# Leaving one low half out of a ternary weight: 23 matmuls in place of 24 in each split product of a decoder kernel

## The reference

```
def _ternary_dequant(w):                       # w is (1024, 1024); groups of 128 along a row
    wg = w.reshape(O, g, 128)
    scale = clip(mean(abs(wg), axis=-1, keepdims=True), 1e-8)
    wn = wg / scale
    q = where(wn > 0.5, 1.0, where(wn < -0.5, -1.0, 0.0))
    return (q * scale).reshape(O, I)
def _bitlinear(x, w): return x @ _ternary_dequant(w).T

x = x + self_attention(layernorm(x), w_q, w_k, w_v, w_o)    # each projection a _bitlinear; rope on q and k
x = x + cross_attention(layernorm(x), ctx, ctx)
x = x + experts(layernorm(x), A, B, Wr, br)
```

## Time and profile before

| | |
|---|---|
| median of 3 runs | 2347.63 us (2345.82 to 2349.23) |
| profiled execution, its own time | 2352.2 us |
| its span in the trace | 2350.4 us |
| granted TensorE clock, mean | 0.97 |
| first half ends, second begins | about 1657 us into the span |

### The profile page before, as it was taken

How to read it: one execution, slowest core, us unless ns; L and a number is a source line. 1 busy time by engine, 2 the same in 40 slices (tenths; PEclk the granted TensorE clock), 3 DMA queues, 4 the chain that set the end, 5 groups by cost and what they waited for, 6 DMA issues and landing times. The chain is left out here.

```text
span 2350.4 us, 52152 instructions
## 1 busy us (share of the span) xinstructions
PE 2135.3 (91%) x19912; PEld 1386.6 (59%) x19912; DVE 1640.3 (70%) x4559; ACT 1143.4 (49%) x2562; POOL 919.3 (39%) x855
## 2 busy tenths in 40 slices
PE   1565999999999999999999999998789998989988
PEld 1343666666666666666666666665445555555544
DVE  9997567667676676676676766655577777777764
ACT  7976433333333333333333333333666766666661
POOL 1111333333333333333333333332555565565650
PEclk9777999999999999999999999998899999999999
DMA  9976555656556555556465555558977868696852
GB/s 243 194 154 146 118 138 129 155 118 149 137 130 136 141 130 142 127 139 146 120 153 133 130 137 138 122 128 219 223 168 171 201 172 206 165 205 155 190 122 68
DMA packets 741961, 358.16 MB, mean 152 GB/s; under 512 B 688200, under 2 KB 688456, under 8 KB 741712
## 3 DMA queue, kind: packets, MB, share of 16 engines
q1 hardware_dynamic: 741712, 354.82, 64.2%
HBM read 104.11 MB, written 49.28 MB: 65 GB/s over the span
## 5 line engine op out<-in xcount | busy, mean ns | idle before, releaser
L819 POOL TENSOR_TENSOR halves<-prob,halves 128x384 f16<-128x384 f32 x256 | 234.6, 916 | 725.1 <-ACT halves L762 725.1
L62 PE MATMUL ps_j<-xT,wT 128*128 128x256 f16 x3744 | 428.3, 275 | 50.6 <-DMA wT<-rows_qkv 50.6
L87 DVE CUSTOM_DVE_ANT_0 prob<-ps_s,mask 128x128 f32<-128x128 f32 (+1 forms) x1024 | 304.6, 353 | 225.3 <-PE ps_s L77 224.2
L62 PEld LDWEIGHTS ps_j<-xT,wT 128*128 128x128 f16 x3744 | 368.8, 99 | 112.5 <-issue 50.6
L93 ACT ACTIVATE prob<-prob,negmax 128x128 f32<-128x128 f32 x512 | 202.0, 395 | 285.0 <-DVE negmax L87 284.8
L939 DVE TENSOR_TENSOR raw<-raw,cos 128x512 f32<-128x512 f32 x128 | 137.9, 1077 | 290.5 <-DMA swp<-raw 290.5
L62 PE MATMUL ps_t<-xT,wT 128*128 128x256 f16 x2400 | 270.2, 273 | 0.0
L62 PEld LDWEIGHTS ps_t<-xT,wT 128*128 128x128 f16 x2400 | 234.5, 98 | 38.2
L94 ACT ACTIVATE prob<-prob,negmax 128x256 f32<-128x256 f32 x512 | 252.9, 494 | 0.0
L1441 POOL TENSOR_TENSOR halves<-prob,halves 128x768 f16<-128x768 f32 x128 | 210.5, 1645 | 91.7 <-ACT halves L1385 91.6
L752 ACT ACTIVATE raw<-ps_j 128x512 f32<-128x512 f32 x78 | 46.4, 595 | 408.9 <-PE ps_j L62 408.9
(11 more groups left out here) (186 smaller groups left out, 3644.9 us busy)
## 6 DMA issues: line engine op xcount, KB each, us to landing
swp<-raw SPq DMA_DIRECT2D x512, 64.0 KB, 2.0
xin<-in_x SPq DMA_DIRECT2D x33, 512.0 KB, 4.2
kv_ahead<-in_ctx SPq DMA_DIRECT2D x16, 1024.0 KB, 5.5
x_kept<-after_self_attention SPq DMA_DIRECT2D x16, 1024.0 KB, 5.6
xres<-in_x SPq DMA_DIRECT2D x31, 512.0 KB, 4.1
after_self_attention<-xres SPq DMA_DIRECT2D x30, 512.0 KB, 3.3
queries<-q2T SPq DMA_DIRECT2D x30, 512.0 KB, 3.1
out<-x SPq DMA_DIRECT2D x10, 1024.0 KB, 4.6
```

What stands on the lines that cost most here:

```text
L62: last = pe.matmul(out, lhs(i, a), rhs(j, a), start=a == 0 and k == 0, stop=a == n_tiles - 1 and k == 2)
L87: dve.tensor_tensor_reduce(scores[:, cols], bank[:, cols], hidden, scale, NO_SCORE, ALU.add, ALU.min, least[:, n:n + 1]).then_inc(done, 1)
L819: pool.tensor_tensor(halves[:, e, 1, :], prob[:, e], halves[:, e, 0, :], ALU.subtract).then_inc(prob_lo, 1)
```

## The change

Each row of a weight matrix is multiplied with a ratio that makes the scale of its first group a float16 number: ratio = float16(256 s0) / (256 s0). The first group then has no low half, a weight tile has 15 blocks and not 16, and a product needs 23 matmuls. The result of a row is divided by its ratio afterwards.

- `ternary(n)`: one operation on 24 values (`bounds`) in place of three of the four of L862, then a reciprocal and a float16 copy of the first scale, their product (`ratio`), the scales times the ratio (`scaleR`), and the reciprocal of the ratio (`factor`). High and low halves of the scales are two operations on GpSimd (`halves_of_scales`), placed in its order beside the tiles.
- `scaled_rows(n)`: 15 activations.
- q and k: `projection` becomes two activations of 256 columns, each with its factor per partition as scale; the rotary tables are divided by 256 once, on GpSimd.
- v and the output product: the factors run along columns there, so they go out to DRAM and come back to all partitions (`store_factors`, `load_factors`, three times), and one more VectorE operation multiplies the bank in PSUM with them (`scaled_values`, the first operation of `add_projection`). `low_values` moves behind `maxima`, `high_values` on ScalarE behind `projection` and the step's first weight tile.
- In SBUF `swp` moves beside `cos` and `sin`, the weights shrink by a sixteenth, and some small tiles are joined.

```diff
-def split_product(pe, out, lhs, rhs, n_tiles, part=None):
+def split_product(pe, out, lhs, rhs, n_tiles, part=None, exact=None):
     for a in part or range(n_tiles):
-        for k, (i, j) in enumerate(((0, 1), (1, 0), (0, 0))):
-            last = pe.matmul(out, lhs(i, a), rhs(j, a), start=a == 0 and k == 0,
-                             stop=a == n_tiles - 1 and k == 2)
+        terms = [t for t in ((0, 1), (1, 0), (0, 0)) if a > 0 or exact is None or t[exact] == 0]
+        for t in terms:
+            last = pe.matmul(out, lhs(t[0], a), rhs(t[1], a), start=a == 0 and t is terms[0],
+                             stop=a == n_tiles - 1 and t == (0, 0))
...
+            def store_factors(k):
+                m, cols, rows = factor_part(k)
+                sp.wait_ge(factor_done, number[2 + m, cols.stop - 1] + 1)
+                with nc.allow_non_contiguous_dma("one column"):
+                    sp.dma_start(factors[m, rows].rearrange("(t p) -> p t", p=P),
+                                 factor_vo[:, m, cols]).then_inc(factor_out, 16)
+            def load_factors(k):
+                m, cols, rows = factor_part(k)
+                sp.wait_ge(factor_out, 16 * (k + 1))
+                sp.dma_start(factor_rows[:, m, rows], factors[m, rows].partition_broadcast(P)) \
+                    .then_inc(factor_in, 16)
...
-                for i, scale in ((0, scaleW), (1, low)):
+                for i, scale in ((0, scaleR), (1, low)):
...
-                    for g in range(NG):
+                    for g in range(i, NG):
...
-                act.activation(raw[:, g % 2].rearrange("p w n -> p (w n)"), bank(("qk", g, 0))[:],
-                               ACT.Copy, scale=1.0 / W_SCALE).then_inc(raw_done, 1)
+                for w in range(2):
+                    last = act.activation(raw[:, g % 2, w], bank(("qk", g, 0))[:, bass.ts(w, T)],
+                                          ACT.Copy, scale=factor_qk[:, w, t:t + 1])
+                last.then_inc(raw_done, 1)
...
+            def halves_of_scales(n):
+                u = n % NS
+                pool.wait_ge(scales_done, n + 1)
+                pool.tensor_tensor(high[:, u, :], bounds[:, u, 0, :],
+                                   ratio[:, u:u + 1].broadcast_to([P, NG]), ALU.mult) \
+                    .then_inc(high_done, 1)
+                pool.wait_ge(high_done, n + 1)
+                pool.tensor_tensor(low[:, u, :], scaleR[:, u, :], high[:, u, :],
+                                   ALU.subtract).then_inc(low_done, 1)
...
+            pool.wait_ge(tables_in, 32)
+            for table in (cos, sin):
+                pool.tensor_scalar(table[:], table[:], 1.0 / W_SCALE, None, ALU.mult) \
+                    .then_inc(tables_done, 1)
...
-                for to, factor, bound in ((scaleW, W_SCALE, ALU.max), (high, W_SCALE, ALU.max),
-                                          (thr[:, :, 0], 0.5, ALU.max),
-                                          (thr[:, :, 1], -0.5, ALU.min)):
-                    dve.tensor_scalar(to[:, u, :], asum[:, u, :], factor / GROUP,
-                                      factor * SCALE_EPS, ALU.mult, bound).then_inc(scaled, 1)
-                dve.wait_ge(scaled, 4 * n + 4)
-                dve.tensor_tensor(low[:, u, :], scaleW[:, u, :], high[:, u, :],
-                                  ALU.subtract).then_inc(low_done, 1)
+                dve.scalar_tensor_tensor(
+                    bounds[:, u], asum[:, u, :].unsqueeze(1).broadcast_to([P, 3, NG]),
+                    SCALE_EPS * GROUP, parts.unsqueeze(2).broadcast_to([P, 3, NG]),
+                    ALU.max, ALU.mult).then_inc(scaled, 1)
+                dve.wait_ge(scaled, n + 1)
+                dve.reciprocal(inverse0[:, u:u + 1], bounds[:, u, 0, 0:1]).then_inc(first_done, 1)
+                dve.tensor_copy(high0[:, u:u + 1], bounds[:, u, 0, 0:1]).then_inc(first_done, 1)
+                dve.wait_ge(first_done, 2 * n + 2)
+                dve.tensor_tensor(ratio[:, u:u + 1], high0[:, u:u + 1], inverse0[:, u:u + 1],
+                                  ALU.mult).then_inc(ratio_done, 1)
+                dve.wait_ge(ratio_done, n + 1)
+                dve.tensor_scalar(scaleR[:, u, :], bounds[:, u, 0, :], ratio[:, u:u + 1], None,
+                                  ALU.mult).then_inc(scales_done, 1)
+                factor = factor_qk[:, m] if m < 2 else factor_vo[:, m - 2]
+                dve.reciprocal(factor[:, t:t + 1], ratio[:, u:u + 1]).then_inc(factor_done, 1)
...
+            def scaled_values(c):
+                half = c[2] % 2
+                dve.wait_ge(j_ready, ready(c))
+                dve.wait_ge(factor_in, 16 * (half + 1))
+                dve.scalar_tensor_tensor(bank(c)[:], bank(c)[:], 1.0 / W_SCALE,
+                                         factor_rows[:, 0, bass.ts(half, BANK)],
+                                         ALU.mult, ALU.mult).then_inc(v_scaled, 1)
...
-                dve.scalar_tensor_tensor(z, bank(c)[:], 1.0 / W_SCALE, z, ALU.mult, ALU.add) \
-                    .then_inc(freed(c)[0], 1)
+                dve.wait_ge(out_scaled, 4 * c[1] + c[2] + 1)
+                dve.tensor_tensor(z, bank(c)[:], z, ALU.add).then_inc(freed(c)[0], 1)
...
-                    low_values(extra[g - 1])
+                    scaled_values(extra[g - 1])
...
                     maxima(g - SCORES)
+                if g - 1 in extra and extra[g - 1][0] == "v":
+                    low_values(extra[g - 1])
```

More of the change, by code:

```diff
@@ L180, in self_attention @@
     stats = sb("stats", [P, 2, 6])
[L181 to L184, removed]
+    small = sb("small", [P, 8])
+    minus_half, nothing = small[:, 0:1], small[:, 1:2]
+    rstd, mv = small[:, 2:3], small[:, 3:5]
+    parts = small[:, 5:8]
     NS = 4
     asum = sb("asum", [P, NS, NG])
-    scaleW = sb("scaleW", [P, NS, NG])
+    bounds = sb("bounds", [P, NS, 3, NG])
+    high0 = sb("high0", [P, NS], F16)
+    inverse0 = sb("inverse0", [P, NS])
+    ratio = sb("ratio", [P, NS])
+    factor_qk = sb("factor_qk", [P, 2, DT])
+    factor_vo = sb("factor_vo", [P, 2, DT])
+    scaleR = sb("scaleR", [P, NS, NG])
     high = sb("high", [P, NS, NG], F16)
     low = sb("low", [P, NS, NG])
-    thr = sb("thr", [P, NS, 2, NG])
     def staging(name, slots, pairs):
@@ L769, in _ @@
             for g in range(GEND):
-                if g - 1 in extra and extra[g - 1][0] == "v":
-                    high_values(extra[g - 1])
                 if 0 <= g - SUMS - 1 < GP:
@@ L777, in _ @@
                     scaled_rows(n)
+                if g - 1 in extra and extra[g - 1][0] == "v":
+                    high_values(extra[g - 1])
                 if 0 <= g - SCORES < GP:
@@ L850, in ternary, with compare @@
                 stage, below, sign, _ = staged(n)
+                m, t = tiles[n]
                 u = n % NS
                 w = stage.rearrange("p (g i) -> p g i", g=NG)
+                def compare(to, k, side):
+                    dve.tensor_tensor(to.rearrange("p (g i) -> p g i", g=NG), w,
+                                      bounds[:, u, k, :].unsqueeze(2)
+                                      .broadcast_to([P, NG, GROUP]), side).then_inc(compared, 1)
                 dve.wait_ge(*weights_loaded(n))
@@ new lines, in ternary @@
+                dve.tensor_scalar(scaleR[:, u, :], bounds[:, u, 0, :], ratio[:, u:u + 1], None,
+                                  ALU.mult).then_inc(scales_done, 1)
+                factor = factor_qk[:, m] if m < 2 else factor_vo[:, m - 2]
+                dve.reciprocal(factor[:, t:t + 1], ratio[:, u:u + 1]).then_inc(factor_done, 1)
+                compare(below, 2, ALU.is_lt)
+                before = n - 2 if n < NQKV else n - 1
+                if before >= 0 and n != NQKV:
+                    dve.wait_ge(halved, 2 * before + 2)
@@ L874, in ternary @@
+                compare(sign, 1, ALU.is_gt)
                 dve.wait_ge(compared, 2 * n + 2)
```

141 lines of the change are left out of this document (95 added, 46 removed).

## The result

The changed kernel takes 2327.37 us (median of 4 runs, 2324.65 to 2333.75) against 2347.77 for the kernel before (4 runs), a ratio of 0.9907 with a 95% interval of 0.9889 to 0.9925. On another chip the same pair gave 0.9924 (0.9906 to 0.9942). The forecast of 2322 and its range hold, but two of its terms were wrong and partly cancelled. The profiled execution took 2324.65, its span is 2322.5.

A forecast was written before the change was run, and what follows sets the result against it. VectorE was taken to bound the start, TensorE the middle stage. Saving -51.0, start +19.6, late rotation +4, seam +1 and second half +1 make -25.4 us: from 2347.6 to 2322, range 2304 to 2340.

The forecast's parts named there:

- Rival 4: Whole kernel: a matmul less gives back no time since weight loads set the pace, leaving only costs, 2373 us; chance 0.01.
- The late rotation (+4): Middle stage: `rotated` has little room, some steps will be late by a few tenths; +4 us, bounds 0 and 17.
- rival 2: Middle stage: GpSimd's subtraction slides, rotation sets the pace, TensorE waits 0.3 us in 56 steps; 17 us, 2335; chance 0.17.
- rival 3: VectorE's turn in every step: rewriting a PSUM bank is slow, about 2370 us at 2.4 us an operation; chance 0.05.
- The start (+19.6): First stage, where VectorE is the path: all additions there, (a) to (e), cost 19.6 us.
- (a): Start, VectorE's chain of small operations: 0.37 us more a tile, 28 tiles, 10.4 us, bounds 6 to 19.
- (b): Start: GpSimd's halves of the scales hold VectorE's compare, 0.25 us a tile, 7.0 us, bounds 0 and 12.4.
- (c): Start: value results need two VectorE operations in place of one, 4.1 us, of which 2.1 counts.
- (d): Start: ScalarE's rows end 0.3 us sooner in three waits, -0.9 us.
- (e): Start: rotary tables divided on GpSimd once, beside compares, 1.0 us, bounds 0 and 2.
- The stores: Start, SyncE's queue: three 4-byte-element stores and three loads cost nothing, hidden by VectorE work; without that about 4 us each.
- Rival 1: Start nearly free: (a) at its lower bound 7, (b) nothing, (c) 2; -43 us in all, 2305; chance 0.13.

The follow-up runs named there:

- only-saving kernel: The kernel before with the first tile's low-half matmul left out of every q, k, value and output product, nothing else changed: 2304.22 us, ratio 0.9791.
- kernel with only the costs: The changed kernel with all 24 matmuls a product again: 2384.42 us, ratio 1.0129 to the kernel before.
- contiguous stores: The changed kernel with factors stored in 16 or 32 bytes per partition, so in another order: 2312.75 us, ratio 0.9819; again 2315.09 us, 0.9833.
- kernel without the ratio's operations: The kernel with contiguous stores, without VectorE's operations for ratio and factor (both set to 1 once): 2303.33 us, ratio 0.9782 to the kernel before.

## Why the prediction was right, and where it was not

**The saving (-51.0) was right.** The only-saving kernel gives 49.6 in all. In the changed kernel 48.5 lie between pairs 12 and 127, 0.42 a step in the mean and 0.43 from pair 51 to 75, where 0.438 was forecast. Columns explain it: 1024 columns in 0.43 us are 0.42 ns each, which is one cycle at 2.4 GHz, the level that the granted clock of 1.00 stands for. Rival 4 fell.

**The late rotation (+4) was over-sized, and rival 2 fell.** In seven or eight of the 114 steps between pairs 12 and 127 the scores wait for `rotated`, about 1 us together (read from the starts in the timeline), and the middle stage is 0.6 us longer than in the only-saving kernel. `projection`'s two activations of 0.468 take 0.84 together, not 0.90, and GpSimd's subtraction did not become the pace. The kernel with only the costs shows a middle stage unchanged to 0.1 us.

**The rewritten bank takes 0.692**, forecast 0.69; rival 3 fell. VectorE has 78 of 100 us, forecast 77.

**The start (+19.6) came out at +22.7, with another make-up.**

- (a), the small operations, had the chain right and its worth too dear: 0.91 in place of 0.54 for a tile, as forecast. Over all 32 tiles the time from the end of the sum to the start of the compare, worked out from the timeline, adds up to 35.5 us after and 23.1 before. But all that VectorE and GpSimd add moves pair 12 by no more than 7.4 to 7.6 us with contiguous stores, less than the 10.4 of (a) alone. The 11.7 us of the kernel without the ratio's operations aren't a measure of the 10.4, since its chain is shorter than that of the kernel before, too.
- (b), "I take 0.25: 28 x 0.25 = 7.0", is a step that failed. The compares keep 1.21 and 1.22 us, and GpSimd's operations wait for them. The earlier trace rows had shown a compare that began 0.06 behind a GpSimd operation and took 1.94; I carried that over to operations that begin behind the compare. The Trainium skill ("SBUF — State Buffer", section "Who interferes with whom") is right in that the two exclude each other and the later one blocks; in this kernel the later one is GpSimd's, so its 12.4 us never arise. Where GpSimd holds the first turn the old picture is seen (timeline of both engines):

```profile
118.52 2.13 POOL L885 TENSOR_TENSOR xh<-xin,xh 128x1024 f16<-128x1024 f32 x1 [4.41 <-ACT xh L792]
...
119.83 0.86 DVE L960 SCALAR_TENSOR_TENSOR bounds<-asum,small 128x24 f32<-128x24 f32 x1
```

- (c), (d) and (e) weren't measured one by one. Of what (a) adds, 4.1 us come back in the compares themselves, which the forecast didn't look for: before, four of them lasted 1.94 to 3.15 us, one of them shown in the earlier trace rows, and now none takes more than 1.23 (without the ratio's operations three take 1.93 again, so it goes by where GpSimd's long operations happen to fall). What is left, 12.4 less 4.1, is 8.3, close to the 7.4 to 7.6 measured, so (c) and (e) can't be large. How (c), (d) and (e) share the small rest stays open.
- The stores, "in SyncE's queue I cost at nothing, hidden by the 10 us of VectorE work between", is the other step that failed. They cost 15.3 us here (22.7 less 7.4, by kernels from two chips) and 21.9 on the second chip (pair 12 at 315.2 less 293.3, both from there). I asked whether the factors come in time, and they do. What isn't hidden is what is in flight or queued behind the store, the transposes above all: they hold the weights, the layer norm tiles and, through the queue's order, the swapped halves on which the scores wait. Even the 4 us of "without that cover about 4 us each" was under half of what the third store cost, 9.4 us: from pair 9 to 12 the changed kernel takes 48.0 us, with contiguous stores 38.6.

**Seam and second half (+1, +1).** The seam measured +0.8. The second half measured -2.9, in a stage where one kernel gave 692 and 699; whether the four results there cost a microsecond stays open.

**The sum.** -48.5 + 22.7 + 0.8 - 2.9 = -27.9 on the profiled pair, forecast -25.4. The timed medians differ by 20.4, and by 17.0 on the second chip. The profiled execution of the changed kernel was the fastest of its four, and the one of the kernel before took 4.4 us more than its median, so the traces show more gain than the medians. That the forecast came so close is luck: what the start adds on VectorE and GpSimd was too dear by 12 (19.6 against 7.4 to 7.6; 7 of it is (b)), the stores too cheap by 15 to 22.

**Rival 1** was more right than its chance of 0.13. The start apart from the stores is as cheap as it had it, and with contiguous stores the ratio of 0.9819 makes 2305 of the kernel before's 2347.77, its very number. That number was reached with a slip, though: "-43" leaves out the +4 of the middle stage, the +1 and +1 of the seam and second half and the +1 of (e), and with them its terms give -36, 2312. Those terms came out near nothing, too.

**What stays open.** Why a store in 4-byte elements takes as long for 512 of them as for 1024, and by what the transfers beside it are held, from another queue too, no run shows. Nor does any tell whether it is the size of the elements or the number of pieces (128 in place of 512 or 1024) that makes the short store fast; the edit changes both. Whether the ratio can be made with a shorter chain wasn't tried.

## What to carry to other kernels

Price a new DMA by what is issued or in flight behind it, not only by when its own data is needed: a 4 KB store can be the dearest line of a change. Price two engines that exclude each other by who begins first, which the order of the instructions around them decides. Run the saving alone and the cost alone: -49.6 and +30.6 add up to -19.0, against the 20.4 and 17.0 measured, and show at once which side has something left to win.

## What the runs showed of the hardware that I had not expected

- A store of 512 or 1024 elements of 4 bytes each lands after 10.9 and 11.9 us; as 16 or 32 bytes of a partition after 3.0 and 1.9. Other transfers wait meanwhile: transposes in the same queue (11.71 us in place of 3.90) and from another (9.8 and 11.0 us of waiting), and ordinary ones too (a load 12.6 us in place of 4.5, a swap's four 9.7 in place of 2.0).
- GpSimd's operation on 8 columns takes 0.20 us alone (the least duration above) and 1.17 begun 0.10 us behind a VectorE compare of 1.21, which isn't slowed.
- VectorE's operation on 512 float32 columns takes 0.69 us, and 1.07 to 1.08 when its SBUF operand has a step of 16 or 32 bytes; a step in PSUM with float16 in SBUF costs nothing (0.687), and a plain copy with such a step takes 0.62.
- One wait of 6.7 us on TensorE is paid beyond itself: the granted clock from 290 to 310 us is 0.83, and 23 matmuls take 6.14 us, where 23 take 5.13 at clock 1.00. With contiguous stores there is no such wait, and the clock of the same stretch is 1.00.
